# Two graph-attention and mixture layers on one core: second layer's products 1536 columns wide beside the last mixture chunk, first routed layer's matrices kept on the chip

## What is computed

```python
x = x + graph0(ln(x))    # 4 heads; softmax over adj == 1 of leaky_relu(src[i,h] + dst[j,h]), times Wh
x = x + mixture0(ln(x))  # 8 experts, 128 -> 512 relu -> 128, weights of the best 2 (softmax of 2 scores)
x = x + graph1(ln(x))    # one attention matrix: softmax over adj > 0 of mean over heads of leaky_relu(s1 + s2)
x = x + mixture1(ln(x))  # h = relu(ln @ Wi.T + bi); twice: h = relu(shared(h) + routed(h) + h); out = h @ Wo.T + bo
```

## Time and profile before

| what | us |
|---|---|
| median of 3 runs (lowest, highest) | 739.09 (736.9, 740.69) |
| the execution that was profiled | 739.58 |
| its span in the trace | 737.8 |
| busy: PE, DVE, ACT, POOL | 617.6, 526.4, 388.4, 164.8 |
| last mixture0 chunk, from the end of L610 to the first routed chunk | 400.7 to 533.9 |
| routed chunks 0 to 2 beside graph1's chunks 1 to 3 | 533.9 to 699.6 |
| last routed chunk | 699.6 to 732.6 |

### The profile page before, as it was taken

How to read it: one execution, slowest core, us unless ns; L and a number is a source line. 1 busy time by engine, 2 the same in 40 slices (tenths; PEclk the granted TensorE clock), 3 DMA queues, 4 the chain that set the end, 5 groups by cost and what they waited for, 6 DMA issues and landing times.

```text
span 737.8 us, 14828 instructions
## 1 busy us (share of the span) xinstructions
PE 617.6 (84%) x5288; PEld 467.8 (63%) x5288; DVE 526.4 (71%) x1071; ACT 388.4 (53%) x761; POOL 164.8 (22%) x130
## 2 busy tenths in 40 slices
PE   2856776999999999899999979984589889889696
PEld 1645664867868678677887636763547647647453
DVE  6699989677677776678663579269597998997300
ACT  1767895777867678567887455431022222222231
POOL 4201032011111111102111113416403603602100
PEclk9977995999999999999999989996769979969888
DMA  7446630011110111101111011010546716716643
GB/s 156 84 79 115 172 58 1 2 59 58 59 58 1 59 58 59 59 2 59 58 59 58 0 58 56 2 45 3 150 136 189 226 58 197 217 57 200 213 130 113
DMA packets 30702, 63.08 MB, mean 86 GB/s; under 512 B 4556, under 2 KB 7636, under 8 KB 30644
## 3 DMA queue, kind: packets, MB, share of 16 engines
q1 hardware_dynamic: 27156, 52.50, 23.5%
q0 software_dynamic: 2624, 9.44, 6.6%
q10 hardware_dynamic: 864, 0.33, 0.2%
HBM read 69.59 MB, written 1.05 MB: 96 GB/s over the span
## 4 chain that ended last, share of the span: by engine, by line
PE 65%; DVE 18%; ACT 7%; issue 5%; POOL 3%; DMA 1%; SPq 1%; DVEq 0%; ACTq 0%
PE bank L598 16%; PE bank L610 12%; PE bank L558 10%; PE bank L679 6%; PE bank L543 5%; PE bank L716 4%; PE bank L709 3%; ACT arena L956 2%; POOL reg_b L455 2%; DVE reg_c L1355 2%; DVE arena L1210 2%; PE bank L534 2%; DVE arena L1198 2%; ACT ysb L913 1%; PE bank L507 1%
## 5 line engine op out<-in xcount | busy, mean ns | idle before, releaser
L956 ACT ACTIVATE arena<-sbc,nd 128x512 bf16<-128x512 f32 x204 | 130.2, 718 | 33.5 <-PE bank L558 33.5
L448 POOL TENSOR_TENSOR x<-x,ysb 128x512 f32<-128x512 f32 x36 | 61.9, 1720 | 304.9 <-ACT ysb L913 300.6
L610 PEld LDWEIGHTS bank<-arena,reg_c 128*128 128x128 f32 x1024 | 116.8, 192 | 7.2 <-issue 7.2
L598 PE MATMUL bank<-hTc,arena 128*128 128x512 f32 x256 | 120.9, 628 | 0.0
L610 PE MATMUL bank<-arena,reg_c 128*128 128x128 f32 x1024 | 116.9, 275 | 0.0
L558 PE MATMUL bank<-reg_b,arena 128*128 128x99 bf16 x2048 | 102.4, 213 | 11.3 <-DVE arena L1210 11.2
L558 PEld LDWEIGHTS bank<-reg_b,arena 128*128 128x128 bf16 x2048 | 100.6, 101 | 14.1 <-issue 12.1
L903 ACT ACTIVATE reg_c<-bank,b 128x512 f32<-128x512 f32 x128 | 87.9, 688 | 36.3 <-PE bank L598 36.3
L1355 DVE SCALAR_TENSOR_TENSOR reg_c<-reg_b,nd,reg_c 128x512 f32<-128x512 f32 x144 | 96.3, 740 | 0.0
L1198 DVE TENSOR_TENSOR arena<-maskT,arena 128x2048 bf16<-128x2048 bf16 x48 | 60.8, 1266 | 49.8 <-ACT arena L956 49.6
L598 PEld LDWEIGHTS bank<-hTc,arena 128*128 128x128 f32 x256 | 51.1, 202 | 64.6 <-issue 64.6
(11 more groups left out here) (164 smaller groups left out, 729.1 us busy)
## 6 DMA issues: line engine op xcount, KB each, us to landing
arena<-in_wrT SPq DMA_DIRECT2D x128, 256.0 KB, 3.0
reg_c<-in_adj POOLq DMA_DIRECT2D x16, 512.0 KB, 5.9
arena<-in_w1T SPq DMA_DIRECT2D x16, 512.0 KB, 3.9
arena<-in_w2T SPq DMA_DIRECT2D x16, 512.0 KB, 4.8
x<-in_x SPq DMA_DIRECT2D x4, 256.0 KB, 4.6
out_x<-x POOLq DMA_DIRECT2D x4, 256.0 KB, 3.8
arena<-in_wsT SPq DMA_DIRECT2D x1, 512.0 KB, 3.7
arena<-in_gW ACTq DMA_DIRECT2D x2, 64.0 KB, 4.0
```

The costliest lines, as they stand in the source:

```text
L448: nc.gpsimd.tensor_tensor(xi, xi, ysb[:, e % 3, :].rearrange("p (t d) -> p t d", d=P), ALU.add).then_inc(s_acc, 1)
L598: mm(bank[b][:, :], w1[:, s, e % 2, c * P:(c + 1) * P], hTc[:, :], start=True, stop=True).then_inc(full[b], 1)
L610: last = mm(bank[b][:, i * P:(i + 1) * P], hid[:, e % 2, c, i * P:(i + 1) * P], w2[:, s, e % 2, c, :], start=(c == 0), stop=(c == HC - 1))
L956: last = af(ind[:, q, 1, j, :], sbc[:, h, :], ACT.Relu, bias=nd[:, q * QT + j, h:h + 1], scale=BIG)
```

## The change

- **Wide products.** Graph1's chunks 0 to 2 of target columns become one product of 1536 columns (`wide_pair`, four slots in `arena`, two source tiles at a time, DVE L1394), and PE multiplies them into four banks (`attend_wide`, L659). Five of eight pairs stand beside the last mixture0 chunk, three behind it. The last 512 columns remain narrow (`last_tiles`, `attend1` L675); two of their 16 tiles stand ahead of the routed chunks, 14 within them.
- **Order around it.** The preparations of chunks 0 to 2 go ahead of nearly all of the last mixture0 chunk, whose experts run one by one (`first`, `second`, one bank for the output). ACT scales the values in place of POOL (`scale_values`). The norms of routed chunks 0 to 2 are made early and in two buffers.
- **First routed layer.** SP loads the 16 matrices of l = 0 once, into columns 0 to 1023 of `maskT` as soon as the wide products have read a tile. ACT reads each group's expert number and copies its matrix into a slot (`select`, four copies per tile, ahead of `turn(i, 0)`). Only l = 1 is still loaded per group, 64 loads.
- **Small things.** No source rows in chunk 3; loops on PE, ACT and DVE are written out; the second layer's bounds are worked out near the start on DVE.

```diff
         w2 = arena[:, 10240:12288].rearrange("p (s e c d) -> p s e c d", s=2, e=2, c=HC)
-        whx1 = arena[:, 0:T * XM].rearrange("p (t k) -> p t k", t=T)
-        prob0 = arena[:, 4096:8192].rearrange("p (s i) -> p s i", s=8)
-        wsel = arena[:, 0:8192].rearrange("p (s k n) -> p s k n", s=2 * L * GT, k=KC)
+        whx1 = arena[:, 0:2 * CT * XM].rearrange("p (s t k) -> p s t k", s=2, t=CT)
+        wide = arena[:, 2048:2048 + 4 * WW].rearrange("p (s i) -> p s i", s=4)
+        kept = maskT[:, :, 0:2 * KC * HID].bitcast(F32)
+        wsel = arena[:, 0:8192].rearrange("p (l s k n) -> p l s k n", l=L, s=2 * GT, k=KC)
         at = [8192]
...
+            for e in range(E1):
+                sp.wait_ge(s_step, e // 2 * 2 * (H - 1) + e % 2 + 1)
+                sp.dma_start(kept[:, e, :], a["wrT"][:, 0, e, :]).then_inc(s_kept, 16)
...
+                    for g in range(GT):
+                        e = sp.value_load(route[0:1, bass.ds(pair * 2 * GT + r * GT + g, 1)], min_val=0,
+                                          max_val=E1 - 1)
+                        if wait:
+                            sp.wait_ge(full[3 + 2 * r], (pair - 1) * (L + 1) + ((BANK5 if r else BANK3) + L))
+                        sp.dma_start(wsel[:, 1, r * GT + g, :, :].rearrange("p k n -> p (k n)").unsqueeze(1),
+                                     a["wrT"][:, 1, bass.ds(e, 1), :]).then_inc(s_sel[r * GT + g], 16)
+            sp.wait_ge(full[3], BANK3)
             select(0, False)
             with sp.Fori(1, T // 2) as pair:
...
-            with pe.Fori(2, C) as c:
-                k.enter(c, 2, per)
-                chunk0((c + 1) % C)
-                k.leave(C - 2, per)
-            def attend1(t, prob=prob, ready=s_prob):
+            for c in range(1, C):
+                chunk0(c)
...
+            def attend_wide(g):
...
+                pe.wait_ge(s_v1, g // 2 + 1)
+                for t in (2 * g, 2 * g + 1):
+                    pe.wait_ge(s_wide, t + 1)
+                    for i in range(WT):
+                        b, o = i // 3, i % 3 * (P + 1)
+                        last = mm(bank[b][:, o:o + P + 1], wide[:, t % 4, i * P:(i + 1) * P], v1[:, t, :],
+                                  start=(t == 0 and i % 3 == 0), stop=(t == T - 1), skip_group_check=True)
+                        if t == T - 1 and i % 3 == 2:
+                            last.then_inc(full[b], 1)
+                if g < T // 2 - 2:
+                    last.then_inc(s_widef, 1)
...
+                if l == 0:
+                    pe.wait_ge(s_copy, k.event("copy"))
...
+            prepare1(0)
+            source_rows1(0)
+            scores(odiv)
+            first(0)
+            prepare1(1)
+            source_rows1(1)
+            prepare1(2)
+            source_rows1(2)
+            first(1)
+            second(0)
+            first(2)
+            second(1)
+            combine(4)
+            first(3)
+            second(2)
+            first(4)
+            second(3)
+            attend_wide(0)
+            first(5)
+            second(4)
+            attend_wide(1)
+            first(6)
+            second(5)
+            attend_wide(2)
+            first(7)
+            second(6)
+            attend_wide(3)
+            second(7)
+            attend_wide(4)
             prepare1(3)
-            for q in range(2, Q):
-                quad(q)
+            source_rows1(3)
+            for g in range(5, T // 2):
+                attend_wide(g)
+            attend1(0)
+            attend1(1)
...
+            def expert_chunk(src, products):
+                ln_transpose(6, src)
                 normalised()
                 pe.wait_ge(s_ohx, k.event("ohx"))
                 hidden(0)
                 for i in range(CT):
                     for l in range(L):
                         layer(i, l)
-                        attend1(QT + 3 * i + 2 * l)
-                        if i == 0 and l == 0:
-                            for h in range(H):
-                                source_row(h, next_rows)
+                        for t in products.get((i, l), ()):
+                            attend1(t)
                         turn(i)
-                        if l == 0:
-                            attend1(QT + 3 * i + 1)
                     if i < CT - 1:
                         hidden(i + 1)
                     output(i)
...
+            expert_chunk(odiv, {(1, 0): (2,), (2, 0): (3,)})
+            expert_chunk(xn, {(0, 0): (4,), (1, 0): (5,), (2, 0): (6,), (3, 0): (7,)})
+            expert_chunk(odiv, {(0, 0): (8,), (0, 1): (9,), (1, 0): (10,), (1, 1): (11,), (2, 0): (12,),
+                                (2, 1): (13,), (3, 0): (14,), (3, 1): (15,)})
+            ln_transpose(6, xn)
...
             def prepare1(c):
...
                 ln_out(c)
-                project(whx1, c)
...
+                    af(nd[:, tiles, h], whx1[:, c % 2, :, P + H + h], ACT.Exp, bias=nmx[:, h:h + 1], scale=-SLOPE)
+                af(v1[:, tiles, P], whx1[:, c % 2, :, XC], ACT.Exp, bias=nmx[:, H:H + 1]).then_inc(s_exp, 1)
+            def scale_values(c):
+                act.wait_ge(s_exp, 3 + c)
+                for i in range(CT):
+                    t = c * CT + i
+                    last = af(v1[:, t, 0:P], whx1[:, c % 2, i, 0:P], ACT.Copy, scale=v1[:, t, P:P + 1])
+                last.then_inc(s_v1, 1)
...
+            prepare1(0)
+            source_rows1(0)
...
+            scale_values(0)
+            first(0)
+            prepare1(1)
+            source_rows1(1)
+            gate()
+            prepare1(2)
+            source_rows1(2)
+            first(1)
+            scale_values(1)
+            second_layer(0, 4)
+            scale_values(2)
+            first(2)
+            second_layer(1, 4)
+            combine(4)
+            for e in range(3, E0):
+                first(e)
+                second_layer(e - 1, 4)
+            second_layer(E0 - 1, 4)
             prepare1(3)
-            sums(3 * (P + 1), P + 1)
+            source_rows1(3)
+            scale_values(3)
+            sums(*[3 * (P + 1)] * (WT // 3), to=reg_b)
...
+            def select(t):
+                for g in range(GT):
+                    e = act.value_load(route[0:1, t * GT + g:t * GT + g + 1], min_val=0, max_val=E1 - 1)
+                    last = af(wsel[:, 0, t % 2 * GT + g, :, :].rearrange("p k n -> p (k n)").unsqueeze(1),
+                              kept[:, bass.ds(e, 1), :], ACT.Copy)
+                last.then_inc(s_copy, 1)
+            act.wait_ge(s_kept, 16 * E1)
+            select(0)
+            for c in range(C - 1):
                 ln_out()
                 hidden(0)
                 for i in range(CT):
                     layer(i)
-                    if i == 0:
-                        source_rows1((c + 1) % 2)
+                    select(c * CT + i + 1)
                     turn(i, 0)
                     layer(i)
-                    if i == CT - 1:
+                    if c == C - 2 and i == CT - 1:
                         sums(3 * (P + 1), P + 1)
                     turn(i, 1)
                     if i < CT - 1:
                         hidden(i + 1)
                     output(i)
-                k.leave(C - 1, per)
...
+                    if i == 0 and l == 0:
+                        select(T - 2)
+                        select(T - 1)
...
+            replicate(1)
+            dve.wait_ge(s_acc, E0 + 1)
+            norm(0, 2 * C - 1)
             merge(C - 1, H - 1)
-            norm(C - 1, 2 * C - 1)
+            norm(C - 1, C, odiv)
+            dve.wait_ge(s_acc, (C - 1) * (E0 + 1))
+            statistics(CT)
+            then(statistics(2 * CT, CT))
+            deviations(2 * CT)
+            dve.wait_ge(ev["hTc"], 2 * C)
+            scale(CT, xn, 0)
+            dve.wait_ge(ev["hTc"], 2 * C + 1)
+            scale(2 * CT, odiv, CT)
             best(C - 1, 2 * C - 1)
             gate(C - 1, 2 * C - 1)
...
+            def products(h, tiles, slots, row, columns, ready):
...
+                for j, t in enumerate(tiles):
+                    p = slots[:, t % slots.shape[1], :]
+                    if h:
+                        dve.wait_ge(s_step, before + j + 1)
+                    last = v.scalar_tensor_tensor(p, row, nd[:, t, h:h + 1], p if h else maskT[:, t, columns],
+                                                  ALU.max, ALU.mult)
+                    last.then_inc(s_step if h < H - 1 else ready, 1)
+                if h < H - 1:
+                    k.event("step", len(tiles))
+            def wide_pair(g):
+                dve.wait_ge(s_exp, 3 + g // 2)
+                if g >= 2:
+                    dve.wait_ge(s_widef, g - 1)
+                for h in range(H):
+                    products(h, (2 * g, 2 * g + 1), wide, rows1[:, h, :], slice(0, WW), s_wide)
+            def last_tiles(first, n):
+                if first >= 8:
+                    dve.wait_ge(s_probf, first // QT - 1)
+                for h in range(H):
```

(27 more changed lines are left out.)

343 lines of the change are left out of this document (119 added, 224 removed).

## The result

The changed kernel is slower. In four runs it takes 783.62 us (783.2 to 783.83), beside 738.07 us (736.9 to 740.69) of the kernel before: a ratio of 1.0616, with a 95% interval from 1.0594 to 1.0637. The prediction was 777 us with a range from 745 to 813.

What follows compares the result with a forecast made beforehand. DVE was to carry the wide products before the routed stage, with ACT's copies opening PE gaps in it. First routed tile 575.0, last norm 733.4, plus 37.0 and 5.2: span 775.6, so 777 us; range 745 to 813.

Steps and rivals of the forecast that it cites:

- Part 1: Ahead of 400.7 us: fewer source rows -3.7, loop pause 1.1, moved bound +2.9; sum -1.9, PE done at 398.8 us.
- Part 2: Last mixture chunk: DVE begins at 429.8, 1.74 us a wide product, first routed tile at 575.0, 41 us given away.
- Part 2, the step that failed: Last mixture chunk: POOL's adds stop fully beside DVE's products, adding 3.7 us to a pause (11.4) and 5.0 before the norm.
- Part 3, c: Routed chunks 0 to 2: each ACT matrix copy costs c = 0.9 us, so a gap of 4.6 and a tile of 10.9.
- low rival: Routed chunks: register loads hide behind the copies, c = 0.64, no clock loss; 756 us, chance 0.22.
- 1.0 + 4c: Routed chunks 0 to 2: PE's gap inside a tile with four ACT copies of c each; 4.6 us.
- Part 3, the clock: Routed chunks 0 to 2: clock 0.9 on 62 us of chained PE work, +7 us.
- The waits at the borders: Borders between routed chunks: POOL's one-hot copy ready only after its last add and store, 1.2 us first, 4.2 second.
- Part 4: Last chunk: 33.0 us before, less 3.0 for weight loads, plus 7.0 for eight copies; 37.0, then 5.2 to the end.
- The faster side: Routed chunks: copies end while PE transposes, c near 0, tile 7.8, POOL gets through; about 719 us, chance 0.10.

Runs made afterwards that it cites:

- e9_two_wide: Changed kernel with products two chunks wide instead of three, the rest 512 wide two tiles at a time, both routed layers' matrices by DMA: 730.63 us.
- e7_short_adds: Changed kernel with GpSimd's nine weighted-output adds of the last mixture chunk cut to 2 of 128 columns per tile: 780.05 us.
- e6b_fill: Changed kernel with four more 128x256 matmuls, never read, ahead of the second layer's wait for the turned copy in every tile: 770.34 us.
- e1_behind: Changed kernel with ACT's four copies put behind each tile's first turned copy, and the last chunk's eight behind both first turned copies: 744.79 us.

## Why the prediction was right

The verdict and its two main terms were right: the change gives away some 40 us before the routed stage (forecast 41, measured 38.0), and gets nothing back in it, since ACT's copies open a gap in every tile. How near the sum came, 777 for 783.62, is in part luck, for in two places errors met. Ahead of the routed stage, stops of 11.5 us for POOL did not come, and DVE's eight pairs took 120.0 us instead of 111.2. In the three chunks, twelve tiles were 10.1 us shorter than forecast, and the clock with what the borders had more took 17.4 us more than its 7.

- **Part 1** said that PE is done with the first layer at 398.8 us; the last second half ends near 397.0 and the first wide product starts at 429.15, predicted 429.8. The term of +2.9 for the bound measured 2.2 on DVE (its first indicator product starts at 43.57 us instead of 41.41). Right.
- **Part 2**, pace: 1.74 us a wide product; where POOL is idle, six take 10.45, so 1.74. Right, and e9_two_wide's six 1024-column ones take 7.26, on the same line. The stage began at 571.87, predicted 575.0.
- **Part 2, the step that failed**: "an add makes no headway while these products run". Nine of nine adds were through within 2.9 us, eight of them beside DVE's products. DVE's pause after pair 1 was 4.93 us and not 11.4, and the norm did not wait 5.0 us for held-back adds. In its place DVE paid about 1.0 us per add, which e7_short_adds took away. The 7.7 us of that pause that were put down to PE don't follow from the terms given either (37 less two pairs, 27.8, is 9.2, and less a whole first half 5.7); measured, PE was through with the first wide products 36.6 us after DVE began. By the Trainium skill, GPSIMD Engine Reference, section Key points, it is contention; the traces show both that and the full stop, the latter in e7_short_adds and in the earlier trace rows. I had taken two stops for a law.
- **Part 3, c**: forecast 0.9, measured 0.64, the value of the low rival, to which the earlier trace rows pointed. Reading SP's cadence as ACT's was the error; in the changed kernel the load is hidden under the copy before it, except for 0.26 us before the first. The Trainium skill, VectorE: DVE Perf Modes, section The TRN2 errata, would give an estimate of 0.61 for it. With c = 0.64 in 1.0 + 4c the tile would be 9.9; at full clock it was 10.06.
- **Part 3, the clock**, the term that was mis-sized: +7. From twelve tiles at 10.06 and the other terms as forecast (8.4, 5.4, 6.8) the stretch would be 141.3 us at full clock; it took 165.7. So about 24 us are clock and what the borders had more, of which e6b_fill alone brought back 15.2. The rows that I went by gave one clock (0.74) for a stretch with PE busy for 14.13 of 20 us; the term took 0.9 all the same. The low rival, 756, fell mostly by this. The waits at the borders, forecast at 1.2 and 4.2, were 2.03 and 5.56.
- **Part 4**: 37.0 us to the last add, measured 38.5; the eight copies make PE wait 5.10 us and no matmul waits for weights. Right, a little low for the clock:

```profile
753.57 2.07 PE L705 MATMUL bank<-arena 128*128 128x256 f32 x4 [5.10 <-ACT arena L1103]
763.61 1.13 PE L705 MATMUL bank<-arena 128*128 128x256 f32 x4 [0.16 <-ACT arena L1091]
```

The same four matmuls take 2.07 us after the wait and 1.13 later: the two levels of TensorE's clock, 1.2 and 2.4 GHz.

- **The faster side** was to decide at c = 0.35. What decided was the place: with c = 0.64 and the copies behind the short copy, e1_behind is within 0.8% of before. The prediction costed the length of what was added to ACT, and not that it could stand one line later.
